# A recurrent column scan on TensorE: wrapped rows from one padded state in 32x32 tiles, and the reset product moved

## The chip, the core and the metric

The kernel is one program on one core of a Trainium2 chip. The metric is device time in microseconds: the median of three runs. TensorE is called PE, VectorE DVE, ScalarE ACT, GpSimd POOL and SyncE SP, as the profile does.

## What is computed

The input x has 16 images of 32 channels, 64 rows and 64 columns, fp32. Four residual stages follow each other; each takes the group-normalised x and adds its result to x: a 3x3 convolution, a recurrent scan over the columns, a spectral product on 16x16 modes, and a product with a full spectrum. The change touches the scan alone:

```python
def _cell(prev_col, cur_col, weight_ih, bias_ih, weight_hh, bias_hh):
    pad = jnp.pad(prev_col, ((0, 0), (1, 1), (0, 0)))
    x = jnp.concatenate([pad[:, :-2], pad[:, 1:-1], pad[:, 2:]], axis=-1)
    i_vals = jnp.einsum('bhk,ok->bho', x, weight_ih) + bias_ih
    h_vals = jnp.einsum('bhc,oc->bho', cur_col, weight_hh) + bias_hh
    r_i, z_i, n_i = jnp.split(i_vals, 3, axis=-1)
    r_h, z_h, n_h = jnp.split(h_vals, 3, axis=-1)
    r = jax.nn.sigmoid(r_i + r_h)
    z = jax.nn.sigmoid(z_i + z_h)
    n = jnp.tanh(n_i + r * n_h)
    return n * z + cur_col * (1.0 - z)
...
x = x + _L1_conv_ref(_gn(x), ...)   # 63 steps of _cell over the 64 columns
```

prev_col is the state after the column before, and each row of it is mixed with the rows above and below it.

## The kernel before

**Layout.** The 128 partitions are four quarters of 32 channels. Image row 4h+q lies in quarter q at position h, so a quarter holds 16 positions (H4) of each image. A neighbouring row is mostly in the neighbouring quarter at the same position. Only for the first and the last quarter does it wrap: row 4h-1 is in quarter 3 at position h-1, row 4h+4 in quarter 0 at position h+1.

**Two halves.** The 16 images are two halves of 8 (h = 0 and 1 in the code, HB = 128 columns each). A half step is one column for one half; there are 2 x 63 = 126, in the order (0,w), (1,w), (0,w+1). Each half has its own PSUM banks 4h to 4h+3, for r, z, the state's part of n, and the column's part of n.

**PE** (half_step, L693) runs from_column (L687) for three gates, then waits for the state, then from_state (L679) for r, n and z, each with its semaphore. Both are four matmuls of 128 rows by 32 columns a gate, one for each quarter of outputs (QUARTERS, L677), with 128 moving columns. The moving operand of quarters 1 and 2 is state; that of quarters 0 and 3 is straddled (L169): a second copy of the state with 17 places an image, whose partitions 0 to 63 are written one place off those of 64 to 127, so that one read at offset 0 or 1 holds the wrapped rows.

**The copies.** POOL writes the partitions 0 to 63 of it from mix and keep (L531), while DVE computes the same difference into state; ACT copies state's partitions 64 to 127 (L1049, state_edges) when state is there. PE's from_state waits for both (sedge_ready, lower_ready).

**DVE** (new_state, L1349) does five operations for each half step: pre1 = r gate x h part (L1352, the reset product), pre2 (L1355), keep (L1360), mix (L1363) and state = mix - keep (L1368). Its loop body has six half steps. **ACT** (scan_step, L1064) does sigmoid of r (L1054), sigmoid of z (L1058), tanh (L1062) and the copy. **POOL** also adds the state into the image (L525). **SP** brings the next column for half of the partitions (L431), once a step, when both halves have used the one before. The loop body of PE has eight half steps, that of ACT four steps.

The order on every engine is written by hand; the engines meet at semaphores only.

Of the kernel before, what the change touches and what calls it, by code (L numbers as in the profile page):

```python
# [80 lines left out]
def program(nc, x, conv_w, conv_b, scan_wi, scan_wh, scan_b, w2, w3, w9, out_b, group_d, const_d, out):  # L81
    ctx = ExitStack()
    with ctx:
        def sem(name):
            return ctx.enter_context(nc.semaphore(name))
# [61 lines left out]
        state = [scan_buf() for _ in range(2)]  # L147

# [16 lines left out]
        straddle_both = spec[:, off:off + 2 * NBR]  # L165
        straddle = [straddle_both[:, h * NBR:(h + 1) * NBR] for h in range(2)]
        off += 2 * NBR

        def straddled(h, q, first):  # L169
            return straddle[h][q].rearrange("p (b h) -> p b h", h=H4 + 1)[:, :, first:first + H4]  # L170
# [55 lines left out]
        sedge_ready = [sem(f"sedge_ready{h}") for h in range(2)]  # L226
        h_sum = [sem(f"h_sum{h}") for h in range(2)]
        lower_ready = [sem(f"lower_ready{h}") for h in range(2)]
        straddle_zeroed = sem("straddle_zeroed")
# [172 lines left out]
        def _(sp):  # L402
# [13 lines left out]
            sp.dma_start(sv[P - C:P, 0:3, 0:C], scan_wi[:, :, 2 * C:3 * C]).then_inc(scan_w_in, 16)  # L416
            sp.dma_start(sv[0:C, 0:3, P - C:P], scan_wi[:, :, 0:C]).then_inc(scan_w_in, 16)
# [67 lines left out]
        def _(pool):  # L485
# [34 lines left out]
            ROWS_01 = slice(0, P // 2)  # L520

            def add_state(h, w):
                col = image[:, h * (B // 2 * ROWS):(h + 1) * (B // 2 * ROWS)] \
                    .rearrange("p (n w) -> p n w", w=W)[:, :, ds(w, 1)]
                nc.gpsimd.tensor_tensor(col, col, state[h].unsqueeze(2), ALU.add).then_inc(added[h], 1)  # L525
# [9 lines left out]
            pool.wait_ge(straddle_zeroed, 1)  # L535
            for h in range(2):
                pool.wait_ge(state_ready[h], 1)
                nc.gpsimd.tensor_copy(straddled(h, ROWS_01, 0), state[h][ROWS_01].rearrange("p (b h) -> p b h", h=H4)
                                      ).then_inc(lower_ready[h], 1)
                add_state(h, 0)  # L540
            with pool.Fori(0, W // 2 - 1) as i:
                for k in range(2):
                    for h in range(2):
                        scan_step(h, i * 2 + (k + 1))
            for h in range(2):
                scan_step(h, W - 1)
# [58 lines left out]
        def _(pe):  # L605
# [363 lines left out]
        def _(act):  # L969
# [75 lines left out]
            ROWS_23 = slice(P // 2, P)  # L1045

            def state_edges(h, w):
                act.wait_ge(state_ready[h], w + 1)
                a(straddled(h, ROWS_23, 1), state[h][ROWS_23].rearrange("p (b h) -> p b h", h=H4),  # L1049
                  ACT.Copy).then_inc(sedge_ready[h], 1)  # L1050

# [22 lines left out]
            act.wait_ge(straddle_zeroed, 1)  # L1074
            state_edges(0, 0)
            for w in range(1, 4):
                scan_step(w)
            with act.Fori(1, W // 4) as i:
                for k in range(4):
                    scan_step(i * 4 + k)  # L1080
# [107 lines left out]
        def _(dve):  # L1188
# [131 lines left out]
            v.memset(straddle_both, 0.0).then_inc(straddle_zeroed, 1)  # L1320
# [23 lines left out]
            for h in range(2):  # L1344
                if h == 1:
                    dve.wait_ge(columns_ready, B)
                v.tensor_copy(state[h], columns[:, h * HB:h * HB + HB]).then_inc(state_ready[h], 1)

            def new_state(h, w):  # L1349
                dve.wait_ge(r_gate[h], w)  # L1350
                dve.wait_ge(h_sum[h], w)
                v.tensor_tensor(pre1[h], gr[h], psum[:, 4 * h + 3, 0:HB], ALU.mult).then_inc(reset_done[h], 1)  # L1352
                dve.wait_ge(reset_done[h], w)
# [4 lines left out]
                dve.wait_ge(lower_ready[h], w)  # L1358

# [10 lines left out]
            with dve.Fori(0, (W - 1) // 3) as i:  # L1370
                for k in range(3):
                    for h in range(2):
                        new_state(h, i * 3 + (k + 1))

# [301 lines left out]
```

## Time and profile before

| | us |
|---|---|
| median of the runs | 573.09 |
| lowest and highest | 572.53 and 574.57 |
| the profiled execution | 571.37 |
| its span, first to last instruction | 569.6 |

What lies around the span is 1.8 us. The page of the profile gives the busy time of each engine and the chain that ended last, that is, the last instruction followed back to what released it. The timeline gives single instructions; a run of equal ones is one line with its count, and its duration reaches from the first start to the last end. An fp32 matmul is two MATMUL instructions and two LDWEIGHTS (PEld). The shape behind an operation on PE (128\*32) is rows by columns of the array, the one after it the moving operand.

### The profile page before, as it was taken

What the parts mean: (1) busy time and instruction counts of PE and PEld (TensorE: products, weight loads), DVE (VectorE), ACT (ScalarE), POOL (GpSimd) and SP (SyncE); (2) the same over time, 40 slices, a digit from 0 to 9 for tenths busy, and PEclk for the clock granted to TensorE, in tenths of its full rate; (3) what the DMA queues carried; (4) which work ended last, traced back from release to release, by engine and by line L of the source; (5) the groups of instructions that cost most, each with busy time, mean ns of one, the idle gap of its engine ahead of it and who ended that gap; (6) DMA issues with size and microseconds to landing.
All of it is one profiled execution on the core that took longest, in us unless ns stands there. A gap on an engine that the chain in (4) does not pass through costs nothing.

```text
span 569.6 us, 28853 instructions
## 1 busy us (share of the span) xinstructions
PE 522.1 (92%) x11502; PEld 415.1 (73%) x11502; DVE 465.2 (82%) x1245; ACT 387.7 (68%) x814; POOL 296.0 (52%) x423
## 2 busy tenths in 40 slices
PE   2999999779999999999999999998989999999995
PEld 2333333467777777777777799997868898999995
DVE  7679885568989898989899879887877897487886
ACT  2545979867777777777777896676748998656541
POOL 7665665046666666666666520211558899522000
PEclk9999999989999999999999999999999999999999
DMA  6920000011111111111111310000308887103334
GB/s 197 412 34 0 2 2 5 1 43 40 41 42 37 46 37 42 41 38 45 37 44 39 121 41 2 1 0 2 96 25 256 264 286 251 51 1 150 148 146 151
DMA packets 26044, 45.82 MB, mean 80 GB/s; under 512 B 5632, under 2 KB 16128, under 8 KB 25104
## 3 DMA queue, kind: packets, MB, share of 16 engines
q1 hardware_dynamic: 24912, 44.98, 24.7%
q8 instruction: 32, 0.52, 0.4%
q10 hardware_dynamic: 672, 0.15, 0.1%
q0 software_dynamic: 416, 0.07, 0.1%
q14 instruction: 12, 0.10, 0.1%
HBM read 28.53 MB, written 8.39 MB: 65 GB/s over the span
## 4 chain that ended last, share of the span: by engine, by line
PE 43%; DVE 31%; issue 11%; ACT 6%; POOL 3%; DMA 3%; DVEq 2%; SPq 0%; ACTq 0%; POOLq 0%
PE psum L619 14%; PE psum L648 8%; DVE spec L1360 8%; PE psum L826 8%; DVE spec L1352 6%; DVE spec L1363 6%; PE psum L786 4%; DVE small L1245 3%; PE psum L932 3%; PE psum L747 2%; POOL work L360 2%; ACT work L302 2%; DVE spec L1355 2%; DMA image<-x_dram 1%; DVE image L1623 1%
## 5 line engine op out<-in xcount | busy, mean ns | idle before, releaser
L683 PE MATMUL psum<-spec,matrices 128*32 128x128 f32 x3024 | 109.3, 278 | 14.2 <-ACT spec L1049 7.3
L683 PEld LDWEIGHTS psum<-spec,matrices 128*32 128x32 f32 x3024 | 76.1, 110 | 46.5 <-ACT spec L1049 46.5
L690 PE MATMUL psum<-spec,matrices 128*32 128x128 f32 x3024 | 107.3, 274 | 1.3 <-DMA spec<-work 1.3
L531 POOL TENSOR_TENSOR spec<-spec 64x128 f32<-64x128 f32 x126 | 70.6, 560 | 71.9 <-DVE spec L1363 71.9
L690 PEld LDWEIGHTS psum<-spec,matrices 128*32 128x32 f32 x3024 | 85.5, 110 | 4.1 <-issue 4.0
L648 PE MATMUL psum<-spec,matrices 128*64 128x512 f32 x384 | 86.2, 606 | 1.0 <-ACT spec L983 1.0
L509 POOL TENSOR_SCALAR spec<-image,small 32x960 f32<-32x960 f32 (+1 forms) x48 | 55.6, 1159 | 34.1 <-PE psum L648 21.7
L826 PE MATMUL psum<-work 128*32 128x128 f32 x2368 | 68.9, 273 | 4.9 <-POOL work L360 2.7
L360 POOL COPY work<-work 32x768 f32<-32x768 f32 x74 | 62.2, 841 | 18.5 <-DVE work L1467 7.3
L826 PEld LDWEIGHTS psum<-work 128*32 128x32 f32 x2368 | 63.9, 110 | 9.3 <-issue 7.4
L525 POOL TENSOR_TENSOR image<-image,spec 128x128 f32 (+1 forms) x128 | 69.4, 542 | 0.0
L360 ACT ACTIVATE work<-work 32x768 f32<-32x768 f32 x74 | 62.4, 843 | 7.6 <-PE psum L826 3.1
L648 PEld LDWEIGHTS psum<-spec,matrices 128*64 128x64 f32 x384 | 27.1, 138 | 53.6 <-issue 50.5
L619 PE MATMUL psum<-kept,work 128*64 128x128 f32 x1024 | 57.0, 273 | 2.4 <-DVE work L396 1.6
L619 PEld LDWEIGHTS psum<-kept,work 128*64 128x64 f32 x1024 | 55.8, 139 | 3.1 <-ACT work L396 1.9
L1360 DVE SCALAR_TENSOR_TENSOR spec<-spec,work 128x128 f32<-128x128 f32 x126 | 54.2, 430 | 0.5 <-ACT spec L1058 0.3
L983 ACT ACTIVATE spec<-image,small 96x1024 f32<-96x1024 f32 (+1 forms) x32 | 39.5, 1234 | 18.1 <-PE psum L648 16.6
L1062 ACT ACTIVATE psum<-spec 128x128 f32<-128x128 f32 x126 | 35.5, 282 | 23.0 <-DVE spec L1355 17.3
L1355 DVE SCALAR_TENSOR_TENSOR spec<-psum,small,spec 128x128 f32<-128x128 f32 x126 | 44.2, 351 | 4.5
L1058 ACT ACTIVATE spec<-psum 128x128 f32<-128x128 f32 x126 | 35.0, 278 | 17.1 <-PE psum L683 17.0
L1054 ACT ACTIVATE spec<-psum 128x128 f32<-128x128 f32 x126 | 35.1, 279 | 15.8 <-PE psum L683 10.2
L1245 DVE BATCH_NORM_STATS2 small<-image 128x6 f32<-128x512 f32 x64 | 40.1, 682 | 5.0 <-DMA image<-x_dram 3.9
(153 smaller groups left out, 819.3 us busy)
## 6 DMA issues: line engine op xcount, KB each, us to landing
work<-w_dram SPq DMA_DIRECT2D x66, 256.0 KB, 3.3
spec<-work SPq DMA_DIRECT2D x124, 64.0 KB, 1.9
image<-x_dram SPq DMA_DIRECT2D x3, 2048.0 KB, 12.7
out_dram<-image SPq DMA_DIRECT2D x3, 2048.0 KB, 7.3
image<-x_dram SPq DMA_DIRECT2D x4, 512.0 KB, 6.0
work<-w_dram SPq DMA_DIRECT2D x1, 2048.0 KB, 8.0
out_dram<-image SPq DMA_DIRECT2D x4, 512.0 KB, 3.8
kept<-const_dram SPq DMA_DIRECT2D x1, 192.0 KB, 5.1
```

Of the source, the lines that this page charges most:

```text
L360: return copy(dst, src, *func)
L509: nc.gpsimd.tensor_scalar(to, of, sc0[j % 2][q, u:u + 1], sh0[j % 2][q, u:u + 1], ALU.mult, ALU.add).then_inc(norm_pool, 1)
L525: nc.gpsimd.tensor_tensor(col, col, state[h].unsqueeze(2), ALU.add).then_inc(added[h], 1)
L531: nc.gpsimd.tensor_tensor(straddled(h, ROWS_01, 0), *of, ALU.subtract).then_inc(lower_ready[h], 1)
L619: last = mm(out[o], stationary[:, o], moving, start=True, stop=True)
L648: last_mm = mm(psum[o, n % 4, :], cv[:, kx, o], rows_[:, 8 * half:8 * half + 8, kx:kx + W], start=kx == 0, stop=kx == 2)
L683: last = mm(psum[QUARTERS[hm], 4 * h + g, 0:HB], sv[:, g, QUARTERS[hm]], moving[hm], start=starts, stop=True)
L690: last = mm(psum[q, 4 * h + g, 0:HB], sv[:, 3 + g, q], e, start=True, stop=stops)
L826: last = mm(o, wt[t // 8][:, t % 8, r, :], pl[:, t, from_:to], start=starts and k == 0 and r == 0, stop=r == 1, skip_group_check=True)
L1245: v.bn_stats(bnv[:, at_:at_ + 6], image[:, ds(j * (GB * ROWS) + 512 * k, 512)]).then_inc(half_sem, 1)
L1355: v.scalar_tensor_tensor(out=pre2[h], in0=psum[:, 4 * h + 2, 0:HB], scalar=bias_s[:, 2:3], in1=pre1[h], op0=ALU.add, op1=ALU.add).then_inc ...
L1360: v.scalar_tensor_tensor(out=keep[h], in0=gz[h], scalar=1.0, in1=columns[:, ds(w * (2 * HB) + h * HB, HB)], op0=ALU.subtract, op1=ALU.mult ...
```

## The change

One padded state for each half replaces state and the second copy. It has 17 places an image and the places between images stay zero; each half has one place more at its front. state(h, q, group) reads it at the image's rows (group 0), one place back (-1) or one on (+1); for group +1 the view starts one place later and drops its first.

from_state then does four matmuls a gate of two shapes: two of 128x64 over all rows (the halves of the outputs, with the weights that do not wrap), and two of 32x32 for the wrapped rows, from quarter 3 to quarter 0 and from quarter 0 to quarter 3, with weights of their own in slot 7 of scan_m. All four go into the same PSUM bank. from_column does two of 128x64 a gate instead of four of 128x32.

The copies on POOL and ACT are gone, with their semaphores. DVE computes the reset product of the other half between mix and state of this half. ACT does the r and z gates of half 0 for the next step after the tanh of half 1. DVE's last three steps stand behind its loop, and so do ACT's.

```diff
-        straddle_both = spec[:, off:off + 2 * NBR]
-        straddle = [straddle_both[:, h * NBR:(h + 1) * NBR] for h in range(2)]
-        off += 2 * NBR
-
-        def straddled(h, q, first):
-            return straddle[h][q].rearrange("p (b h) -> p b h", h=H4 + 1)[:, :, first:first + H4]
+        state_both = spec[:, off:off + 2 * (NBR + 1)]
+        off += 2 * (NBR + 1)
+
+        def state(h, q=slice(0, P), group=0):
+            if group == 1:
+                at_ = h * (NBR + 1) + 1
+                return state_both[q, at_:at_ + NBR].rearrange("p (b h) -> p b h", h=H4 + 1)[:, :, 1:]
+            at_ = h * (NBR + 1)
+            return state_both[q, at_:at_ + NBR].rearrange("p (b h) -> p b h", h=H4 + 1)[:, :, 1 + group:1 + group + H4]
...
-            sp.dma_start(sv[P - C:P, 0:3, 0:C], scan_wi[:, :, 2 * C:3 * C]).then_inc(scan_w_in, 16)
-            sp.dma_start(sv[0:C, 0:3, P - C:P], scan_wi[:, :, 0:C]).then_inc(scan_w_in, 16)
+            for q, of in ((slice(P - C, P), slice(2 * C, 3 * C)), (slice(0, C), slice(0, C))):
+                sp.dma_start(sv[q, 7, 0:3 * C].rearrange("p (g c) -> p g c", c=C), scan_wi[:, :, of]).then_inc(scan_w_in, 16)
...
-            def scan_step(h, w):
-                pool.wait_ge(mix_ready[h], w)
-                pool.wait_ge(keep_ready[h], w)
-                of = [t[h][ROWS_01].rearrange("p (b h) -> p b h", h=H4) for t in (mix, keep)]
-                nc.gpsimd.tensor_tensor(straddled(h, ROWS_01, 0), *of, ALU.subtract).then_inc(lower_ready[h], 1)
-                pool.wait_ge(state_ready[h], w + 1)
-                add_state(h, w)
...
+            HALVES = (slice(0, P // 2), slice(P // 2, P))
+
             def from_state(h, g, starts=False):
 
-                moving = (straddled(h, slice(0, P), 0), state[h], state[h], straddled(h, slice(0, P), 1))
-                for hm in (1, 2, 0, 3):
-                    last = mm(psum[QUARTERS[hm], 4 * h + g, 0:HB], sv[:, g, QUARTERS[hm]], moving[hm],
-                              start=starts, stop=True)
+
+                for o in HALVES:
+                    mm(psum[o, 4 * h + g, 0:HB], sv[:, g, o], state(h), start=starts, stop=False, skip_group_check=True)
+                for to, of, group in ((0, slice(P - 32, P), -1), (3, slice(0, 32), 1)):
+                    last = mm(psum[QUARTERS[to], 4 * h + g, 0:HB], sv[of, 7, C * g:C * g + C], state(h, of, group),
+                              start=False, stop=True, skip_group_check=True)
                 return last
 
             def from_column(h, g, parity, stops=False):
-                up, lo = edges_of(h, parity)
-                for q, e in zip(QUARTERS, (up, up, lo, lo)):
-                    last = mm(psum[q, 4 * h + g, 0:HB], sv[:, 3 + g, q], e, start=True, stop=stops)
+                for o, e in zip(HALVES, edges_of(h, parity)):
+                    last = mm(psum[o, 4 * h + g, 0:HB], sv[:, 3 + g, o], e, start=True, stop=stops, skip_group_check=True)
                 return last
...
-                pe.wait_ge(sedge_ready[h], w)
-                pe.wait_ge(lower_ready[h], w)
+                pe.wait_ge(state_ready[h], w)
                 from_state(h, 0).then_inc(r_sum[h], 1)
...
-            def scan_step(w):
-                reset_gate(0, w)
-                update_gate(0, w)
-                state_edges(1, w - 1)
+            def scan_step(w, last=False):
                 candidate(0, w)
                 reset_gate(1, w)
                 update_gate(1, w)
-                state_edges(0, w)
                 candidate(1, w)
+                if not last:
+                    reset_gate(0, w + 1)
+                    update_gate(0, w + 1)
...
-            def new_state(h, w):
+            def reset(h, w):
                 dve.wait_ge(r_gate[h], w)
                 dve.wait_ge(h_sum[h], w)
                 v.tensor_tensor(pre1[h], gr[h], psum[:, 4 * h + 3, 0:HB], ALU.mult).then_inc(reset_done[h], 1)
+
+            def new_state(h, w, last=False):
+
                 dve.wait_ge(reset_done[h], w)
...
                 v.tensor_tensor(mix[h], gn[h], gz[h], ALU.mult).then_inc(mix_ready[h], 1)
+                if not last:
+                    reset(1 - h, w + h)
                 dve.wait_ge(mix_ready[h], w)
                 dve.wait_ge(keep_ready[h], w)
                 dve.wait_ge(added[h], w)
-                dve.wait_ge(sedge_ready[h], w)
-                v.tensor_tensor(state[h], mix[h], keep[h], ALU.subtract).then_inc(state_ready[h], 1)
+                v.tensor_tensor(state(h), by_image(mix[h]), by_image(keep[h]), ALU.subtract).then_inc(state_ready[h], 1)
```

## Rows read from the trace of the kernel before

**Rows 1.** Page, part 1: busy time, share of the span and instructions of each engine.
```profile
PE 522.1 (92%) x11502; PEld 415.1 (73%) x11502; DVE 465.2 (82%) x1245; ACT 387.7 (68%) x814; POOL 296.0 (52%) x423
```

**Rows 2.** Page, part 4: chain that ended last, by engine and by line.
```profile
PE 43%; DVE 31%; issue 11%; ACT 6%; POOL 3%; DMA 3%; DVEq 2%; SPq 0%; ACTq 0%; POOLq 0%
PE psum L619 14%; PE psum L648 8%; DVE spec L1360 8%; PE psum L826 8%; DVE spec L1352 6%; DVE spec L1363 6%; PE psum L786 4%; DVE small L1245 3%; PE psum L932 3%; PE psum L747 2%; POOL work L360 2%; ACT work L302 2%; DVE spec L1355 2%; DMA image<-x_dram 1%; DVE image L1623 1%
```

**Rows 3.** Views by line of L1352 and L690: duration ns minimum/median/maximum, first and last start.
```profile
L1352 DVE TENSOR_TENSOR spec<-spec,psum x126: 277/279/289, 117.1 to 320.3; 128x128 f32<-128x128 f32 x126
...
L690 PE MATMUL psum<-spec,matrices x3024: 269/273/421, 110.8 to 319.1; 128*32 128x128 f32 x189
```

**Rows 4.** Timeline of all engines, 202.4 to 206.3: start, duration, engine, line [idle before].
```profile
202.47 0.84 PE L690 MATMUL psum<-spec,matrices 128*32 128x128 f32 x24
...
202.72 0.28 DVE L1352 TENSOR_TENSOR spec<-spec,psum 128x128 f32<-128x128 f32 x1
203.02 0.31 ACT L1049 ACTIVATE spec<-spec 64x128 f32<-64x128 f32 x1
203.04 0.35 DVE L1355 SCALAR_TENSOR_TENSOR spec<-psum,small,spec 128x128 f32<-128x128 f32 x1
...
203.30 0.46 DVE L1360 SCALAR_TENSOR_TENSOR spec<-spec,work 128x128 f32<-128x128 f32 x1
...
203.38 0.86 PE L683 MATMUL psum<-spec,matrices 128*32 128x128 f32 x24
...
203.74 0.29 DVE L1363 TENSOR_TENSOR spec<-psum,spec 128x128 f32<-128x128 f32 x1
203.87 0.28 ACT L1054 ACTIVATE spec<-psum 128x128 f32<-128x128 f32 x1 [0.17 <-PE psum L683]
...
204.06 0.84 PE L690 MATMUL psum<-spec,matrices 128*32 128x128 f32 x24
204.06 0.29 DVE L1368 TENSOR_TENSOR spec<-spec 128x128 f32<-128x128 f32 x1
204.10 0.56 POOL L531 TENSOR_TENSOR spec<-spec 64x128 f32<-64x128 f32 x1 [0.49 <-DVE spec L1363]
204.27 0.28 DVE L1352 TENSOR_TENSOR spec<-spec,psum 128x128 f32<-128x128 f32 x1
...
205.61 0.29 DVE L1368 TENSOR_TENSOR spec<-spec 128x128 f32<-128x128 f32 x1
...
206.19 0.29 DVE L1352 TENSOR_TENSOR spec<-spec,psum 128x128 f32<-128x128 f32 x1 [0.30 <-issue]
```

**Rows 5.** Groups of instructions, 117 to 321: count | busy, mean ns | idle before, releasers.
```profile
L683 PEld LDWEIGHTS psum<-spec,matrices 128*32 128x32 f32 x3000 | 75.6, 110 | 42.4 <-ACT spec L1049 42.4
```

**Rows 6.** Timeline of PE, 337.9 to 346, then its first two steps alone.
```profile
338.20 7.21 PE L786 MATMUL psum<-matrices,work 128*64 128x128 f32 x128
345.34 0.46 PE L795 MATMUL psum<-matrices,work 128*32 128x32 f32 x32
...
338.20 0.44 PE L786 MATMUL psum<-matrices,work 128*64 128x128 f32 x4
```

**Rows 7.** Timeline of PE at three changes of shape: the end of the old shape.
```profile
338.00 0.27 PE L747 MATMUL psum<-kept,work 128*128 128x128 f32 x1
...
344.91 0.50 PE L786 MATMUL psum<-matrices,work 128*64 128x128 f32 x6
...
82.64 0.53 PE L667 MATMUL psum<-kept,spec 128*32 128x128 f32 x6
83.09 0.65 PE L648 MATMUL psum<-spec,matrices 128*64 128x512 f32 x2
```

**Rows 8.** Timeline of PE at the end of its loop body, 145.2 to 147.2.
```profile
145.33 0.86 PE L683 MATMUL psum<-spec,matrices 128*32 128x128 f32 x24
146.12 0.86 PE L690 MATMUL psum<-spec,matrices 128*32 128x128 f32 x24
```

**Rows 9.** Stretch 117.1 to 121.0: busy us (instructions) of each engine, granted clock, DMA.
```profile
117.10:121.00 3.90, 3.31 (x72) 3.18 (x72) 2.11 (x8) 1.46 (x6) 1.07 (x2) 0.59 0.22 53
```

More of the change, by code:

```diff
@@ L145, in scan_buf @@
             return spec[:, off - HB:off]
-        state = [scan_buf() for _ in range(2)]
         upper_e = spec[:, off:off + 4 * HB]
@@ L164, in program, with by_image @@
         NBR = B // 2 * (H4 + 1)
-        straddle_both = spec[:, off:off + 2 * NBR]
-        straddle = [straddle_both[:, h * NBR:(h + 1) * NBR] for h in range(2)]
-        off += 2 * NBR
-        def straddled(h, q, first):
-            return straddle[h][q].rearrange("p (b h) -> p b h", h=H4 + 1)[:, :, first:first + H4]
+        state_both = spec[:, off:off + 2 * (NBR + 1)]
[6 more added lines that the diff above has]
+            return state_both[q, at_:at_ + NBR].rearrange("p (b h) -> p b h", h=H4 + 1)[:, :, 1 + group:1 + group + H4]
+        def by_image(buf):
+            return buf.rearrange("p (b h) -> p b h", h=H4)
         columns = work[:, 0:B * ROWS]
@@ L225, in program @@
         state_ready = [sem(f"state_ready{h}") for h in range(2)]
-        sedge_ready = [sem(f"sedge_ready{h}") for h in range(2)]
         h_sum = [sem(f"h_sum{h}") for h in range(2)]
-        lower_ready = [sem(f"lower_ready{h}") for h in range(2)]
-        straddle_zeroed = sem("straddle_zeroed")
+        state_zeroed = sem("state_zeroed")
         r_sum, z_sum, n_sum = [[sem(f"{g}_sum{h}") for h in range(2)] for g in "rzn"]
@@ L519, in _ @@
             pool.wait_ge(norm_pool, 3 * B)
-            ROWS_01 = slice(0, P // 2)
             def add_state(h, w):
+                pool.wait_ge(state_ready[h], w + 1)
                 col = image[:, h * (B // 2 * ROWS):(h + 1) * (B // 2 * ROWS)] \
-                    .rearrange("p (n w) -> p n w", w=W)[:, :, ds(w, 1)]
-                nc.gpsimd.tensor_tensor(col, col, state[h].unsqueeze(2), ALU.add).then_inc(added[h], 1)
-            def scan_step(h, w):
-                pool.wait_ge(mix_ready[h], w)
-                pool.wait_ge(keep_ready[h], w)
-                of = [t[h][ROWS_01].rearrange("p (b h) -> p b h", h=H4) for t in (mix, keep)]
-                nc.gpsimd.tensor_tensor(straddled(h, ROWS_01, 0), *of, ALU.subtract).then_inc(lower_ready[h], 1)
-                pool.wait_ge(state_ready[h], w + 1)
-                add_state(h, w)
-            pool.wait_ge(straddle_zeroed, 1)
+                    .rearrange("p (b h w) -> p b h w", h=H4, w=W)[:, :, :, ds(w, 1)].rearrange("p b h o -> p b (h o)")
+                nc.gpsimd.tensor_tensor(col, col, state(h), ALU.add).then_inc(added[h], 1)
             for h in range(2):
-                pool.wait_ge(state_ready[h], 1)
-                nc.gpsimd.tensor_copy(straddled(h, ROWS_01, 0), state[h][ROWS_01].rearrange("p (b h) -> p b h", h=H4)
-                                      ).then_inc(lower_ready[h], 1)
                 add_state(h, 0)
@@ L543, in _ @@
                     for h in range(2):
-                        scan_step(h, i * 2 + (k + 1))
+                        add_state(h, i * 2 + (k + 1))
             for h in range(2):
-                scan_step(h, W - 1)
+                add_state(h, W - 1)
             pool.wait_ge(t_done, 8)
@@ L1042, in _ @@
                     bias=sh1[:, GB - 1:GB]).then_inc(columns_ready, 1)
[L1045 to L1050, printed above, removed]
             def reset_gate(h, w):
@@ L1070, in scan_step @@
                 update_gate(1, w)
-                state_edges(0, w)
                 candidate(1, w)
[L1074 to L1078, printed above, removed]
+                if not last:
+                    reset_gate(0, w + 1)
+                    update_gate(0, w + 1)
+            reset_gate(0, 1)
+            update_gate(0, 1)
+            with act.Fori(0, (W - 4) // 4) as i:
                 for k in range(4):
-                    scan_step(i * 4 + k)
+                    scan_step(i * 4 + (k + 1))
+            for w in range(W - 3, W):
+                scan_step(w, w == W - 1)
             act.wait_ge(added[0], W)
@@ L1319, in _ @@
             dve.wait_ge(small_in, 16 * 8)
-            v.memset(straddle_both, 0.0).then_inc(straddle_zeroed, 1)
+            v.memset(state_both, 0.0).then_inc(state_zeroed, 1)
             v.memset(bias_z, 0.0).then_inc(bias_spread, 1)
@@ L1346, in _ @@
                     dve.wait_ge(columns_ready, B)
-                v.tensor_copy(state[h], columns[:, h * HB:h * HB + HB]).then_inc(state_ready[h], 1)
-            def new_state(h, w):
+                dve.wait_ge(state_zeroed, 1)
+                v.tensor_copy(state(h), by_image(columns[:, h * HB:h * HB + HB])).then_inc(state_ready[h], 1)
+            def reset(h, w):
                 dve.wait_ge(r_gate[h], w)
@@ L1357, in new_state @@
                 dve.wait_ge(z_gate[h], w)
-                dve.wait_ge(lower_ready[h], w)
                 v.scalar_tensor_tensor(out=keep[h], in0=gz[h], scalar=1.0, in1=columns[:, ds(w * (2 * HB) + h * HB, HB)],
@@ L1366, in new_state @@
                 dve.wait_ge(added[h], w)
-                dve.wait_ge(sedge_ready[h], w)
-                v.tensor_tensor(state[h], mix[h], keep[h], ALU.subtract).then_inc(state_ready[h], 1)
-            with dve.Fori(0, (W - 1) // 3) as i:
+                v.tensor_tensor(state(h), by_image(mix[h]), by_image(keep[h]), ALU.subtract).then_inc(state_ready[h], 1)
+            reset(0, 1)
+            with dve.Fori(0, (W - 1) // 3 - 1) as i:
                 for k in range(3):
@@ L1373, in _ @@
                         new_state(h, i * 3 + (k + 1))
+            for w in range(W - 3, W):
+                for h in range(2):
+                    new_state(h, w, (h, w) == (1, W - 1))
             dve.wait_ge(added[0], W)
```

## The prediction, made before the changed kernel was run

> **What bounds the kernel now.** I start with the page. Its header counts put PE at 92% of the span, but a share is no bound [rows 1]; the chain that ended last gives PE 43% and DVE 31%, and in it four DVE lines of the scan (L1352, L1355, L1360, L1363) come to 22% [rows 2]. So some stretch is held by DVE. The first and last start of L1352 give its place: 117.1 to 320.3, 203.2 us for 126 half steps, 125 intervals of 1.626 [rows 3]. The timeline of one half step shows how it is held [rows 4]. DVE starts L1352, L1355, L1360, L1363, L1368 at 202.72, 203.04, 203.30, 203.74, 204.06 and the next L1352 at 204.27: 1.55 us with no hole. At the end of its loop body (every sixth half) the next one starts at 206.19, and 0.37 us is added: 105 x 1.55 + 20 x 1.92 = 201.2, and about 2 us more at the cold start make the 203.2. PE in the same period runs from_column in 0.91 with a wait at its end, and from_state in 0.68 (203.38 to 204.06): about 1.33 of work in 1.59. It then waits, and the wait is for ACT's copy L1049, 42 us in all over the scan [rows 5]. **The scan is bound by DVE's issue, and PE has only about 0.26 us of room per half step.** Whatever the change puts on PE beyond that is paid in full, 125 times.
>
> **What PE does per matmul.** Each fp32 matmul is two instructions: 24 for the 12 matmuls of from_state. Matmuls of all columns of the array go side by side: 24 instructions of 32 columns from 203.38 to 204.06 are six steps of four. The 128 instructions of 64 columns at L786 take 7.14 us to the start of the next shape: 64 steps of two [rows 6]. Three numbers come from there.
> - A step where the shape stays the same. The two ends of the L786 block are odd: the first step lasts 0.16 (four instructions end at 338.20 + 0.44, one takes 0.273 [rows 3 and 6], so the second pair started at 338.37), the last one 0.20. The other 62 have 7.14 - 0.36 = 6.78, so **0.109 a step**, for a whole array of 128 moving columns, whatever the cut.
> - A step at which the shape changes. In three places (128x128 to 128x64, 128x64 to 128x32, 128x32 to 128x64) the new shape starts 0.07 to 0.08 us before the last of the old one ends: 338.20 against 338.27, 345.34 against 345.41, 83.09 against 83.17 [rows 6 and 7]. Within one shape the next step starts 0.16 before that end. With 0.273 for an instruction, a change costs **0.203 for the step instead of 0.109: +0.094**.
> - The step after a change: 0.16 for 64 columns (+0.054, above). For 32 columns, from_state after a wait has 0.68 - 5 x 0.109 = 0.135 (+0.025) [rows 4].
>
> These rows agree with the Trainium skill, page TensorEngine Tiling (Array Packing), section Tiling Modes, which says that changing the tiling mode, and not just the tile, drains TensorE. That page speaks against this change.
>
> **The change on PE.** from_column becomes 2 matmuls of 128x64 a gate for 4 of 128x32: six steps as before, 0.654. from_state keeps 4 matmuls a gate, but they are no longer four column strips of one pass over the array: two of 128x64 already fill it (two steps), and the two wrapped 32x32 tiles, (rows 96-127, columns 0-31) and (rows 0-31, columns 96-127), need the same columns of the array again, with N = 128: two further steps if both run side by side. No row of before has a 32-row tile; the nearest is 32 columns, and there a step is 0.109, which I take (the moving side has the same 128 columns). So 4 steps a gate for 2: steps per half are 6 + 12 = 18, 1.962 us, for 12. Then the shape changes twice a gate, to 32x32 and back, six times a half step: 6 x 0.094 = 0.564, and behind them 3 x 0.054 + 3 x 0.025 = 0.237. **PE needs 1.962 + 0.564 + 0.237 = 2.763 us per half step.** Bounds: 1.962 if a change of shape that keeps to other rows is free, about 2.53 if only the weight load behind a change is hidden; above, 3.14 if the first and second instructions of large and small matmuls alternate (four changes a gate: 18 x 0.109 + 12 x 0.094 + 0.054), or 3.09 if the two small tiles overlap only by half (one step more a gate). Below 1.31 there is nothing; that end belongs to the rival where small tiles hide.
>
> **The change elsewhere.** All of this is beside PE, as long as PE needs over 1.6.
> - DVE: the same five operations, with the other half's reset between mix and state, so that two waits for an own result fall away. Starts that depend on the operation before are 0.32 apart (202.72 to 203.04), the independent 204.06 to 204.27 is 0.21: at best some 0.2 per half step is saved [rows 4]. It is hidden under PE's 2.76. The waits that come with it: state(h) is queued behind reset(1-h), which waits for the other half's r gate. In PE time: from_state of the other half starts at S; its r gate now has four steps (0.109 + 0.203 + 0.134, then 0.273), about 0.8 with the hop to ACT (0.49 now, 203.38 to 203.87), then sigmoid 0.28, reset, and state starts at S + 1.33 and ends at S + 1.62. PE wants that state after from_state and from_column, at S + 2.76: 1.1 us of slack, so this wait does not bind. Queued behind it are pre2, keep and mix of the other half, which wait for n_sum and z_sum of S, about then or later, anyway.
> - ACT loses L1049 (0.31 per half); its three gates need 0.84 of 2.76. POOL loses L531 (0.56) and keeps its add L525, which now reads the state with a stride of 17. Strided writes of state by DVE: even twice the 0.29 would be covered. Cover for all of it is PE; without it the DVE chain would again set the pace.
> - SP: the two corner DMAs go to slot 7, the same bytes, early. The column DMAs wait for both h_sum and have 5.5 us per step where now 3.2 do.
> - The first memset is 2 columns longer: nothing. The first half step loses an ACT copy and a POOL copy, under 1 us, inside the cold start.
>
> **The sum.** First to last L1352 after: 125 x 2.763 = 345.4. PE's loop edge, now half hidden: from_state takes 0.79 for 0.68 there (145.33 to 146.12) [rows 8], taken as 0.13 x 15 = 2.0. The clock is at its lower level (1.2 of 2.4 GHz) for part of the first 3.9 us, mean 0.59 [rows 9]; work bound by PE loses 3.9 x 0.41 = 1.6 there. Together 349.0, for 203.2 now: +145.8. At the end of the scan z's last step starts 1.85 after the last from_state (0.649 + 0.703 + 0.163 + 0.203 + 0.134) and ends at 2.13, and with sigmoid, tanh, mix and state (0.28, 0.28, 0.32, 0.29 and the hops) that is 3.4 us instead of 2.5 (203.38 to 205.90): +0.9. **+146.7 us.** The profiled execution has 571.37, which gives 718.1; the median of the runs is 573.09, 1.7 above it, and that gives **719.8**.
>
> **Rivals.**
> 1. *Changing shape is free here* (the 32x32 tiles are seen as parts of the same cut). 1.962 per half: 245.3 + 2.0 + 1.6 - 203.2 + 0.5 = +46, **619**. Against it: every change of shape in the rows pays, 64 to 32 columns among them. Part of it free (the load behind it hidden) is 2.53, about 690, within my main case; an effect of one direction only would give about 660.
> 2. *Large and small alternate instruction by instruction, or the small ones do not pair*: 3.09 to 3.14, 125 x 0.33 to 0.38 more than the forecast, **760 to 767**. The rows show that equal neighbours run in steps of four or two with their first instructions together, so some interleaving exists; whether it reaches across shapes they can't show.
> 3. *Small tiles hide beside the large ones* and PE needs 12 steps, 1.31. Then the loop state, PE, r gate, reset of the other half, state decides: 0.29 + 0.05 + 0.49 + 0.28 + 0.03 + 0.21 = 1.35 for 1.55 now, 125 x 0.2 = 25 less, **548, faster**. It decides from the point at which PE's work per half is below 1.55, that is less than 0.24 us for all six small tiles and changes. For it speaks only that four strips of 32 columns share one step; against it, that the two large tiles cover all rows and columns. The Trainium skill, page TensorE: Matmul & The Clock Gate, Part 3, has 32x32 tiles at different positions overlap with a few ns between their starts; by that rule, if it held beside larger tiles, this rival would be the outcome. No row here has 32-row tiles.
> 4. That the change does not do what it says (the reset not between, the copies still there) is not open: the diff moves the instructions themselves.
>
> **How the numbers follow.** Forecast (690 to 730) 0.60; rival 2 0.14; between rival 1 and the forecast 0.08; rival 1 0.12; rival 3 0.06. The range 640 to 772 holds the forecast, rival 2 and the in-between, 0.82, and leaves out rivals 1 and 3. Faster by over 0.5% (about what a measurement of this kernel can tell from no change) is rival 3: 0.06; within 0.5%: 0.01; slower: 0.93.
>
> **What would show it.** In the profile after: PE without waits for ACT or DVE in the scan, L1352's starts 2.76 apart, from_state 128x64 and 32x32 groups in turn with 0.20 between the last of one and the first of the other, 0.109 within; sigmoid of r about 0.8 after from_state starts; DVE idle about half of the time, waiting for PE. If steps of the small tiles were shorter than 0.109, or overlapped with large ones, I am too high; if the granted clock falls in the scan, too low.

## The result, and the profile after

| | before | changed |
|---|---|---|
| median of the runs, us | 573.25 | 751.63 |
| lowest and highest, us | 572.53 and 574.57 | 737.66 and 767.88 |
| profiled execution, us (span) | 571.37 (569.6) | 737.66 (735.9) |
| its granted clock over the span | 0.995 | 0.963 |

The ratio is 1.295, with a 95% interval of 1.282 to 1.309: slower by 29.5%, where +25.6% was forecast. The ratios here and in the table of experiments compare only the runs that lie near the fastest of their kernel (here 737.66 and 748.49); the two medians as they stand give 1.311, that is +31.1%. The four runs of the changed kernel lie 30 us apart, and they do so in the order of PE's mean granted clock (0.963, 0.947, 0.935, 0.918 for 737.66, 748.49, 754.78, 767.88). The profile below is the fastest of them. The median before, 573.25, is of four runs; 573.09 is that of three of them.

The page of the changed kernel first: busy time, PE's clock in 40 slices, the chain by engine and by line. They answer to [rows 1] and [rows 2].

```profile
PE 701.9 (95%) x9990; PEld 478.3 (65%) x9990; DVE 447.0 (61%) x1245; ACT 336.4 (46%) x687; POOL 230.7 (31%) x295
...
PEclk9999996559999999999999999999999999999999
...
PE 82%; DVE 7%; ACT 5%; issue 2%; POOL 2%; DMA 1%; DVEq 0%; SPq 0%; POOLq 0%; ACTq 0%
PE psum L678 18%; PE psum L676 17%; PE psum L684 15%; PE psum L610 11%; PE psum L639 6%; PE psum L819 5%; PE psum L779 3%; DVE small L1230 3%; PE psum L925 2%; PE psum L740 2%; ACT work L305 2%; ACT work L363 2%; POOL work L363 1%; PE psum L605 1%; DVE image L1615 1%
```

The three matmul lines of the scan, L678 (32x32), L676 (128x64 from the state) and L684 (from_column), now hold half of the span, where the scan's DVE lines held 22%. DVE went from 31% of the chain to 7%. And PEclk shows 6, 5, 5 from 110 to 166 us of the span, where the scan starts; before, it was:

```profile
PEclk9999999989999999999999999999999999999999
```

These are two separate effects: what a half step costs, and the clock at the start of the scan.

**The half step.** The timeline of PE over one half step (start, duration, engine, line, shape, count):

```profile
250.03 0.39 PE L684 MATMUL psum<-spec,matrices 128*64 128x128 f32 x4
250.25 0.39 PE L676 MATMUL psum<-spec,matrices 128*64 128x128 f32 x4
250.56 0.41 PE L678 MATMUL psum<-spec,matrices 32*32 32x128 f32 x4
250.90 0.44 PE L676 MATMUL psum<-spec,matrices 128*64 128x128 f32 x4
251.27 0.41 PE L678 MATMUL psum<-spec,matrices 32*32 32x128 f32 x4
251.61 0.44 PE L676 MATMUL psum<-spec,matrices 128*64 128x128 f32 x4
251.98 0.41 PE L678 MATMUL psum<-spec,matrices 32*32 32x128 f32 x4
252.32 0.88 PE L684 MATMUL psum<-spec,matrices 128*64 128x128 f32 x12
253.03 0.28 PE L676 MATMUL psum<-spec,matrices 128*64 128x128 f32 x2
```

from_state starts at 250.25 and the next one at 253.03: 2.78 us, with no wait for DVE or ACT. The gates stand 0.65, 0.71 and 0.71 apart, and from_column takes 0.71; the prediction's steps give 0.649, 0.703, 0.703 and 0.708. The instruction counts show how two matmuls of a shape share their steps: the small pair is 4 instructions in 0.41, that is two steps, 0.13 between their starts and 0.28 for the last to end. The changes of shape are the gaps from the start of a group's second step to the start of the next group: the second step of the group at 250.25 starts at 250.36 (0.28 before its end at 250.64), the small group at 250.56, so 0.20 here.

On the other engines, in the same stretch (the idle time before an operation and what ended it, in brackets):

```profile
250.08 0.29 DVE L1347 SCALAR_TENSOR_TENSOR spec<-spec,work 128x128 f32<-128x128 f32 x1 [0.69 <-ACT spec L1044]
250.29 0.29 DVE L1350 TENSOR_TENSOR spec<-psum,spec 128x128 f32<-128x128 f32 x1
...
251.02 0.28 ACT L1040 ACTIVATE spec<-psum 128x128 f32<-128x128 f32 x1 [0.77 <-PE psum L678]
...
251.33 0.29 DVE L1338 TENSOR_TENSOR spec<-spec,psum 128x128 f32<-128x128 f32 x1 [0.75 <-ACT spec L1040]
251.54 0.29 DVE L1356 TENSOR_TENSOR spec<-spec 128x128 f32<-128x128 f32 x1
```

The r gate's sigmoid starts 0.77 after from_state (251.02 for 250.25; 0.8 was worked out). The other half's reset product (L1338) comes between mix (L1350) and state (L1356) as the diff says, and waits there 0.75 us. State ends at 251.83, 1.58 us after that from_state started, and PE asks for it 2.78 after: the wait that came with the new order binds nothing. Where before DVE had no hole in a half step [rows 4], it now stands idle for half of it.

**The clock.** Two waits of PE at the start of the scan, three stretches of it (length, busy us and instructions of PE, PEld, DVE, ACT, POOL, then the granted clock, DMA share and GB/s), and the reset product's first and last start, to be set against [rows 3] and [rows 9]:

```profile
113.84 0.44 PE L676 MATMUL psum<-spec,matrices 128*64 128x128 f32 x4 [1.67 <-DVE spec L1333]
...
118.15 1.55 PE L684 MATMUL psum<-spec,matrices 128*64 128x128 f32 x12 [0.94 <-DMA spec<-work]
...
114.00:118.00 4.00, 3.21 (x24) 1.15 (x22) 0.95 (x4) 3.51 (x6) 1.03 (x2) 0.53 0.07 16
118.00:160.00 42.00, 41.85 (x312) 23.82 (x312) 11.28 (x43) 6.43 (x26) 4.37 (x8) 0.50 0.07 17
168.00:484.00 316.00, 316.00 (x4102) 189.66 (x4100) 151.09 (x570) 84.00 (x341) 62.12 (x114) 1.00 0.10 23
...
L1338 DVE TENSOR_TENSOR spec<-spec,psum x126: 286/289/290, 117.2 to 484.6; 128x128 f32<-128x128 f32 x126
```

A half step has 36 matmul instructions. From 118 to 160 there are 312, that is 8.7 half steps of 4.85 us, at the lower level of 1.2 GHz; from 168 on one takes 2.77 at 2.4 GHz. In the kernel before, the clock was low in the scan only within the first 3.9 us [rows 9]. From the first to the last L1338 it is 367.3 us; 125 x 2.777 are 347.1, and the low stretch is the other 20. In the trace it lasts 51 us, from 114.2 to 165.4.

### The profile page after: what moved, and what is told of

Same layout as the page of the kernel before. It is cut to its first block, busy times and chain, and to the rows that moved or that the text cites. A ratio compares the mean times of both kernels' runs of the same rounds, so it can differ in the third digit from the quotient of the medians.

```text
span 735.9 us, 25048 instructions
## 1 busy us (share of the span) xinstructions
PE 701.9 (95%) x9990; PEld 478.3 (65%) x9990; DVE 447.0 (61%) x1245; ACT 336.4 (46%) x687; POOL 230.7 (31%) x295
## 4 chain that ended last, share of the span: by engine, by line
PE 82%; DVE 7%; ACT 5%; issue 2%; POOL 2%; DMA 1%; DVEq 0%; SPq 0%; POOLq 0%; ACTq 0%
PE psum L678 18%; PE psum L676 17%; PE psum L684 15%; PE psum L610 11%; PE psum L639 6%; PE psum L819 5%; PE psum L779 3%; DVE small L1230 3%; PE psum L925 2%; PE psum L740 2%; ACT work L305 2%; ACT work L363 2%; POOL work L363 1%; PE psum L605 1%; DVE image L1615 1%
## 5 line engine op out<-in xcount | busy, mean ns | idle before, releaser
L676 PE MATMUL psum<-spec,matrices 128*64 128x128 f32 x1512 | 167.7, 302 | 1.7 <-DVE spec L1333 1.7
L678 PE MATMUL psum<-spec,matrices 32*32 32x128 f32 x1512 | 161.5, 291 | 0.0
L676 PEld LDWEIGHTS psum<-spec,matrices 128*64 128x64 f32 x1512 | 85.7, 142 | 56.1 <-issue 54.2
L684 PE MATMUL psum<-spec,matrices 128*64 128x128 f32 x1512 | 117.1, 293 | 0.9 <-DMA spec<-work 0.9
L684 PEld LDWEIGHTS psum<-spec,matrices 128*64 128x64 f32 x1512 | 85.1, 143 | 27.8 <-issue 27.7
L1338 DVE TENSOR_TENSOR spec<-spec,psum 128x128 f32<-128x128 f32 x126 | 36.3, 288 | 108.6 <-ACT spec L1040 108.6
L678 PEld LDWEIGHTS psum<-spec,matrices 32*32 32x32 f32 x1512 | 54.0, 105 | 69.7 <-issue 69.7
L1347 DVE SCALAR_TENSOR_TENSOR spec<-spec,work 128x128 f32<-128x128 f32 x126 | 36.8, 292 | 85.9 <-ACT spec L1044 85.9
L639 PEld LDWEIGHTS psum<-spec,matrices 128*64 128x64 f32 x384 | 27.2, 139 | 53.8 <-issue 50.5
```

The lines of the kernel that those rows point to most:

```text
L639: last_mm = mm(psum[o, n % 4, :], cv[:, kx, o], rows_[:, 8 * half:8 * half + 8, kx:kx + W], start=kx == 0, stop=kx == 2)
L676: mm(psum[o, 4 * h + g, 0:HB], sv[:, g, o], state(h), start=starts, stop=False, skip_group_check=True)
L678: last = mm(psum[QUARTERS[to], 4 * h + g, 0:HB], sv[of, 7, C * g:C * g + C], state(h, of, group), start=False, stop=True, skip_group_check ...
L684: last = mm(psum[o, 4 * h + g, 0:HB], sv[:, 3 + g, o], e, start=True, stop=stops, skip_group_check=True)
L1347: v.scalar_tensor_tensor(out=keep[h], in0=gz[h], scalar=1.0, in1=columns[:, ds(w * (2 * HB) + h * HB, HB)], op0=ALU.subtract, op1=ALU.mult ...
```

## Experiments

Every kernel was timed in turns with the kernel before on the same chip (573.9 to 574.6 us there). Half steps are the mean distance of the reset product's starts in the second half of the scan.

| run | median us | ratio (95%) | half step | clock |
|---|---|---|---|---|
| e1_grouped | 652.40 | 1.140 (1.134 to 1.146) | 2.237 | 0.995 |
| e2_no_small | 546.72 | 0.953 (0.949 to 0.957) | 1.398 | 0.993 |
| e3_no_small_old_order | 574.86 | 1.003 (1.001 to 1.005) | 1.618 | 0.993 |
| e4_one_cut | 617.68 | 1.076 (1.073 to 1.079) | 1.969 | 0.995 |
| e5_old_order | 732.92 | 1.273 (1.266 to 1.280) | 2.777 | 0.901 |
| e6_warm | 718.62 | 1.252 (1.247 to 1.258) | 2.777 | 0.996 |
| e7_small_pair | 598.78 | 1.043 (1.039 to 1.047) | 1.795 | 0.990 |
| e8_same_pair | 574.93 | 1.001 (0.998 to 1.004) | 1.612 | 0.991 |
| e9_body_7 | 572.93 | 0.997 (0.9945 to 0.9997) | 1.60 | 0.991 |

The clock is that of the profiled execution; for e5_old_order that was the slowest of its five runs, 781.5 us.

### Steps or changes of shape: e1_grouped and e4_one_cut

The changed kernel with the small matmuls of all three gates behind the large ones (from_state keeps the large ones alone):

```diff
+            def wrapped(h, g):
                 for to, of, group in ((0, slice(P - 32, P), -1), (3, slice(0, 32), 1)):
...
-                from_state(h, 0).then_inc(r_sum[h], 1)
-                from_state(h, 2, True).then_inc(n_sum[h], 1)
-                from_state(h, 1).then_inc(z_sum[h], 1)
+                from_state(h, 0)
+                from_state(h, 2, True)
+                from_state(h, 1)
+                wrapped(h, 0).then_inc(r_sum[h], 1)
+                wrapped(h, 2).then_inc(n_sum[h], 1)
+                wrapped(h, 1).then_inc(z_sum[h], 1)
```

> The changed kernel with its matmuls in another order: in each half step the large (128x64) matmuls of all three gates first, then the small (32x32) ones of all three. As many steps of PE as before, but the shape changes twice a half step and not six times. Theory (PE's steps and its changes of shape are the time): 18 x 0.109 + 2 x 0.094 + 0.054 + 0.025 = 2.23 us a half step instead of 2.78; 571.4 - 203.2 + 125 x 2.23 + 1.6 + 1 = about 649 us, more if PE's clock is low for longer than 3.9 us. Rival (the small matmuls are themselves slow, the change of shape is not): 2.78 again, 718 or more. Second rival (the later r gate now decides: state 0.29, hop 0.05, r group 1.2, sigmoid 0.31, reset to state 0.21): 2.1, below PE's 2.23, so not seen.

The timeline of PE in e1_grouped:

```profile
249.86 0.83 PE L676 MATMUL psum<-spec,matrices 128*64 128x128 f32 x12
250.62 0.85 PE L680 MATMUL psum<-spec,matrices 32*32 32x128 f32 x12
251.40 0.88 PE L686 MATMUL psum<-spec,matrices 128*64 128x128 f32 x12
252.10 0.82 PE L676 MATMUL psum<-spec,matrices 128*64 128x128 f32 x12
```

2.24 us a half step (249.86 to 252.10), 2.237 on average: the same instructions as in the changed kernel, in another order, and 0.54 less. Four changes of shape fewer, so 0.135 for each, of which the prediction had 0.094 in the step and 0.054 or 0.025 in the one behind it. That the small matmuls are slow in themselves is out: e1_grouped has as many of them. The kernel takes 652.4 us for 649.

And with one shape everywhere; the weights of the wrapped rows are padded with zeros over all 128 rows, and from_column has its four matmuls of 128x32 a gate as before. In from_state:

```diff
...
+                for q in QUARTERS:
+                    mm(psum[q, 4 * h + g, 0:HB], sv[:, g, q], state(h), start=starts, stop=False, skip_group_check=True)
+                for i, (to, group) in enumerate(((0, -1), (3, 1))):
+                    at_ = 7 * P + 3 * C * i + C * g
+                    last = mm(psum[QUARTERS[to], 4 * h + g, 0:HB], scan_m[:, at_:at_ + C], state(h, slice(0, P), group),
+                              start=False, stop=True, skip_group_check=True)
```

> The changed kernel with every matmul of the scan in one shape, 128x32: four for the rows that don't wrap, two for the wrapped ones (weights padded with zeros over 128 rows, read from the same padded state one place back or on). As many steps of PE as the changed kernel, no change of shape. Theory: 18 x 0.109 = 1.962 us a half step: 571.4 - 203.2 + 245.3 + 1.6 + 0.5 = 616 us. Rival (a small matmul hides part of a step that a full one does not): the half step is above 1.962 by that part, up to 2.78 if the steps themselves were the whole cost.

1.969 us a half step for 1.962, and 617.7 us for 616. It computes the same as the changed kernel, with no change of shape, and is 0.81 us a half step shorter: 2.777 - 1.969 = 0.808, over six changes 0.135 each, the same price as from e1_grouped. What is left above the kernel before, 1.969 for 1.61, is six more steps over the array (0.65 us) less PE's room (0.26): 0.39 by these numbers, 0.36 measured. The three half steps, 1.969, 2.237 and 2.777 with none, two and six changes, lie on one line; so a 32x32 tile costs the array as much time as a 128x32 one full of zeros.

### What the rest of the change is worth: e2 and e3

e2_no_small drops the loop over the small matmuls in from_state, so it leaves the wrapped rows out of the computation. e3_no_small_old_order does that and puts the reset product back:

```diff
             def new_state(h, w, last=False):
 
+                reset(h, w)
                 dve.wait_ge(reset_done[h], w)
...
-                if not last:
-                    reset(1 - h, w + h)
...
-            reset(0, 1)
```

> The changed kernel without its small matmuls: the wrapped rows are left out of the computation. PE has 12 steps a half step, 1.31 us. Theory: the rest of the change is a gain that PE hides; the loop state, PE, r gate, reset of the other half gives 1.35 us a half step and 20 loop edges of DVE at about 0.37: 571.4 - 25 = about 546 to 550 us. Rival (the new order of DVE or the strided state costs something of its own): 571 us or more.

> The changed kernel without its small matmuls (wrapped rows left out of the computation) and with DVE's old order: the reset product of a half first in its own half step. Theory: DVE's issue sets the pace again as in the kernel before, 1.55 us a half step and the loop edges: 569 to 572 us. The difference to the run without small matmuls in the new order is what the moved reset product is worth: about 22 to 25 us. Rival (the missing copies alone are worth the gain): both runs equal, near 548.

546.7 and 574.9 us. With PE at 12 steps the new order makes the kernel 4.7% faster than the one before; with the old order everything else in the change together (no copies, the padded state, 128x64 tiles) brings nothing, if anything a loss of 0.3%. So the moved reset product is worth 28 us, (1.618 - 1.398) x 125 = 27.5, and only where PE lets it. Whether it would be worth that with the copies still there was not tried. DVE in e2_no_small and, below, in e3_no_small_old_order:

```profile
200.87 0.29 DVE L1334 TENSOR_TENSOR spec<-spec,psum 128x128 f32<-128x128 f32 x1
201.08 0.29 DVE L1352 TENSOR_TENSOR spec<-spec 128x128 f32<-128x128 f32 x1
201.29 0.34 DVE L1340 SCALAR_TENSOR_TENSOR spec<-psum,small,spec 128x128 f32<-128x128 f32 x1
201.55 0.28 DVE L1343 SCALAR_TENSOR_TENSOR spec<-spec,work 128x128 f32<-128x128 f32 x1
201.98 0.29 DVE L1346 TENSOR_TENSOR spec<-psum,spec 128x128 f32<-128x128 f32 x1 [0.15 <-ACT psum L1044]
202.22 0.29 DVE L1334 TENSOR_TENSOR spec<-spec,psum 128x128 f32<-128x128 f32 x1
```

```profile
201.07 0.29 DVE L1347 TENSOR_TENSOR spec<-psum,spec 128x128 f32<-128x128 f32 x1
201.40 0.29 DVE L1351 TENSOR_TENSOR spec<-spec 128x128 f32<-128x128 f32 x1
201.60 0.28 DVE L1334 TENSOR_TENSOR spec<-spec,psum 128x128 f32<-128x128 f32 x1
201.92 0.35 DVE L1341 SCALAR_TENSOR_TENSOR spec<-psum,small,spec 128x128 f32<-128x128 f32 x1
202.19 0.37 DVE L1344 SCALAR_TENSOR_TENSOR spec<-spec,work 128x128 f32<-128x128 f32 x1
202.62 0.29 DVE L1347 TENSOR_TENSOR spec<-psum,spec 128x128 f32<-128x128 f32 x1
```

In the new order reset, state and pre2 start 0.21 apart; in the old one mix to state and reset to pre2 are 0.33 and 0.32 apart. 1.35 us for 1.55 in these rows.

The same question on the changed kernel itself, PE holding:

> The changed kernel with DVE's old order (each half's reset product in its own half step), everything else as changed. Theory: PE holds 2.78 us a half step and hides DVE's order: the same half step at full clock within 0.01 us, so the same time as the changed kernel but for the clock (715 at a clock as in the kernel before, up to 768 as its runs were). Rival (the wait of state for the other half's reset binds): shorter by up to 0.2 us a half step, 25 us.

Its half step is 2.777 us, to the nanosecond that of the changed kernel: neither the gain nor the new wait of the reordering is to be seen. The median (732.9, runs from 723 to 782, the slowest above the 768 that were expected at most) is the clock's, below.

### The clock: e6_warm

```diff
+                if nth is None and h == 0:
+                    for _ in range(20):
+                        mm(psum[:, 4, 0:P], group_m, group_m, start=True, stop=True)
                 pe.wait_ge(state_ready[h], w)
                 from_state(h, 0).then_inc(r_sum[h], 1)
```

> The changed kernel with 20 further matmuls (128x128, result unused) where PE waits for the first state before the first from_state. Theory (PE's idle time there lets its clock fall to the lower level, and the pattern of short gaps after it keeps it low for 50 us and more): the clock stays at its upper level, 1.0 in all stretches of the scan, 2.78 us for every half step and about 713 to 717 us, with runs closer together. Rival (the pattern of the scan itself, with a drained array six times a half step, lets the clock fall): the clock falls all the same, 735 to 768.

718.6 us for 713 to 717, the four runs within 3.6 us. The 20 matmuls take 4.7 us, longer than the wait that they fill, so PE no longer waits for the first state. The same stretches in e6_warm:

```profile
114.00:118.00 4.00, 4.00 (x43) 2.77 (x44) 0.87 (x3) 2.24 (x4) 0.55 (x1) 1.00 0.19 47
118.00:160.00 42.00, 42.00 (x550) 25.33 (x550) 19.91 (x75) 11.36 (x47) 8.21 (x15) 1.00 0.11 27
...
L1341 DVE TENSOR_TENSOR spec<-spec,psum x126: 286/288/289, 116.8 to 463.9; 128x128 f32<-128x128 f32 x126
```

The clock does not fall, and the scan takes 347.1 us from its first to its last reset product. So it is PE's idle time at the start of the scan that brings it down, and not the pattern of the scan. In the changed kernel the clock falls at 114.2, right behind the wait of 1.67 us before the first from_state; in the profiled execution of e5_old_order it falls at 117.1, inside the wait for the column's DMA, 2.1 us there and 0.94 in the changed kernel. In e6_warm PE waits at neither place, so which of the two waits would be enough alone is not shown. But once the clock was low, it stayed low for long in this pattern: 51 us in the changed kernel, 150 us in the profiled execution of e5_old_order, with PE busy in the records but for the DMA wait. Of e5_old_order, then of e1_grouped:

```profile
118.00:260.00 142.00, 142.00 (x1056) 79.81 (x1058) 41.79 (x147) 21.38 (x87) 15.76 (x29) 0.50 0.06 15
272.00:528.00 256.00, 256.00 (x3322) 153.46 (x3318) 131.35 (x461) 68.20 (x277) 50.57 (x93) 1.00 0.10 23
...
118.00:160.00 42.00, 42.00 (x654) 35.00 (x656) 22.18 (x88) 14.73 (x54) 11.51 (x17) 0.97 0.13 32
```

In their profiled executions e1_grouped (two changes a half step) and e4_one_cut (none) fall at the start of the scan as well, at 117.4 and 118.7, and are back after 3.4 us; e7_small_pair (two) and e8_same_pair (none) are back after 6.8.

The four runs of the changed kernel bear out what the low clock costs: since the rows show two levels alone, (1 - mean clock) x 2 x span is the time at the lower one over the whole execution, 54 us in the fastest run and 126 us in the slowest, and a microsecond at that level loses 1 - 2.777 / 4.86 = 0.43: 31 us between the two, where 30.2 were measured.

That the changes of shape are what delays the return fits these rows, but is not shown. By the same formula the nine runs of the changed kernel and e5_old_order have 20 to 154 us at the lower level, and all other runs of the experiments, the kernel before among them, 3 to 24, but for one: a run of e9_body_7, whose scan has one shape, took 613.0 us at a mean clock of 0.850, that is 183 us. So a long low stretch came without changes of shape too, if rarely; where in that run it lay is not on record. Why the scan's pattern is enough to hold the upper level and mostly not to regain it soon was not settled.

### PE's room in the kernel before: e7 and e8

```diff
                 from_column(h, 0, parity)
+                for q in (slice(0, 32), slice(P - 32, P)):
+                    mm(psum[q, 4 * h + 3, 256:256 + HB], sv[q, 7, 0:C], bias_z[q], start=True, stop=True)
                 from_column(h, 1, parity)
```

e8_same_pair has sv[:, 7, 0:C] and bias_z there, all 128 rows, the shape of its neighbours.

> The kernel before with one pair of 32x32 matmuls added to each half step, between the first and the second gate of from_column; their result goes to unused PSUM. They add two steps and two changes of shape to PE: 2 x 0.109 + 2 x 0.094 + 0.05 = 0.456 us, where PE has 0.26 us of room. Theory: PE becomes the bound at 1.335 + 0.456 = 1.79 us a half step for 1.626 with loop edges: +20 us, 592. Rival (small tiles hide beside others, or a change of shape is free): at most 0.22 of added work, inside the room, 573.

> The kernel before with one pair of 128x32 matmuls (the shape of all others in the scan) added to each half step at the same place, result unused. Two steps, 0.218 us, no change of shape; PE has 0.26 us of room. Theory: hidden, 573 to 575 us. Rival (PE's room is smaller than the timeline shows, since the wait of from_state for the copy is what ends it): up to +0.22 us a half step, 600.

One pair of small tiles costs 24.5 us, one pair of full ones 0.6, which is nothing (interval 0.998 to 1.004). PE in e7_small_pair:

```profile
250.73 0.43 PE L690 MATMUL psum<-spec,matrices 128*32 128x128 f32 x8
251.09 0.41 PE L703 MATMUL psum<-spec,matrices 32*32 32x128 f32 x4
251.43 0.64 PE L690 MATMUL psum<-spec,matrices 128*32 128x128 f32 x16
251.89 0.84 PE L683 MATMUL psum<-spec,matrices 128*32 128x128 f32 x24
252.54 0.40 PE L690 MATMUL psum<-spec,matrices 128*32 128x128 f32 x8
```

1.79 us a half step was worked out, 1.795 is measured. Of the 4.5 us above the expected 20, 2 to 3 come from the subtraction: 1.626 for the kernel before holds the slow start of the scan, and 1.79 does not; over the second half of the scan the kernel before takes 1.610, and 125 x (1.795 - 1.610) is 23. The rest was not traced.

### A version that might beat both: e9_body_7

```diff
-            with dve.Fori(0, (W - 1) // 3) as i:
-                for k in range(3):
+            with dve.Fori(0, (W - 1) // 7) as i:
+                for k in range(7):
                     for h in range(2):
-                        new_state(h, i * 3 + (k + 1))
+                        new_state(h, i * 7 + (k + 1))
```

> The kernel before with DVE's scan loop in 9 turns of 14 half steps instead of 21 turns of 6. At each loop edge DVE loses 0.37 us in the trace of the kernel before. Theory (the edge is a fixed price): 12 edges fewer, -4.4 us, 569 us where the kernel before has 573.5. Rival (the edge is dearer for a longer body, or PE and ACT then fill what DVE leaves): 573.

572.9 us for 574.6: 0.3% faster, and the interval (0.9945 to 0.9997) only just leaves out 1. Eleven of the twelve runs lie between 569.6 and 575.2; the twelfth is the one of 613.0 above. Twelve edges are gone, but in the profiled execution the eight that are left cost about 0.42 instead of 0.37, and nearly half of the other half steps take 1.59 instead of 1.55, so more than half of the 4.4 us comes back; what holds them was not taken apart. It is the only one that computes everything and is at all faster than the kernel before, so no version that clearly beats it was found. A from_state in 64x32 tiles, rows 0 to 63 and 64 to 127 apart, was not tried.

## Why the prediction was right

The mechanism was right, and so was the half step (2.763 us for 2.777 measured); the time is right with some luck. The median of 751.6 lies above 690 to 730, the band of the forecast with its chance of 0.60. It lies within 640 to 772 only because that range left room for rival 2, and rival 2 did not happen: what filled the room is the clock, which the prediction names in its last sentence as a sign of being too low and gives, beyond the first 3.9 us, neither a price nor a chance.

- **What bound the kernel** (DVE's issue, 1.55 us, and PE with 0.26 us of room): right. e8_same_pair puts 0.22 us of steps into that room for nothing, e7_small_pair 0.456 and pays the excess, 1.795 for 1.79.
- **18 steps of 0.109** (1.962): e4_one_cut measures 1.969. The step taken over from 128x32 for a tile of 32 rows, the one term without a row of before, held (by the line through e4_one_cut, e1_grouped and the changed kernel).
- **Six changes of shape** (0.564 and 0.237 behind them, 0.80): 0.808 from e4_one_cut, 0.54 for four of them from e1_grouped (0.53 by the same numbers). The rows behind this were changes of column width; it holds for a change of rows too. The Trainium skill (TensorEngine Tiling (Array Packing), section Tiling Modes) says that a change of tiling mode drains the array; all of these agree, and 0.135 us is its price here.
- **2.763 a half step**: 2.777.
- **The cover** (the reordering hidden, the wait of state not binding): e5_old_order, no difference; the moved reset product is worth 28 us without the cover (e2 against e3), where 25 were worked out. With it rival 3 is priced: 548 given, 546.7 measured, had the small tiles been free.
- **Rival 1** (619) is what e4_one_cut has, 617.7: steps without changes. **Rival 2** did not come: the small pair shares its two steps, and large and small do not alternate instruction by instruction.
- **The term that was mis-sized is the clock at the start.** I had 3.9 us at a mean of 0.59 as in the kernel before, 1.6 us of loss; the profiled execution had 51 us at the lower level, about 21 of loss, and other runs up to 126 us over the whole execution. That is nearly all of the 19.6 us between 718.1 and the profiled 737.66, and more in the median. I had seen the fall in [rows 9] and asked only what the same 3.9 us would cost a PE that is bound, not whether the new pattern would end it as soon. With the clock held up (e6_warm) the kernel takes 718.6 for a forecast of 719.8. How long the low stretch lasts, and so where between 737.7 and 767.9 a run ends, stays open.
- Two small terms were off, one each way: the 2.0 us for PE's loop edges did not show (half steps of 2.77 to 2.78 at the upper level all along; the durations read for it, 0.79 and 0.68, would give 0.11 an edge and 1.7 us), and the end of the scan cost about 2 us and not 0.9 (251.3 us from the last reset product to the end of the span, for 249.3).

## What to carry to other kernels

Before matmuls are cut into smaller tiles, count PE's passes over the array and the changes of tile shape in the order of issue: a small tile takes the array's time of a large one with as many moving columns, and each change costs a little more than a further step (0.135 us for 0.109 here). If shapes must mix, group them, or pad the small weights with zeros to the shape of the neighbours. A gain on one engine is worth what the next engine's room allows, here 0.26 us a half step, and that room can be measured beforehand by adding a matmul whose result nobody reads. And where PE's clock falls in a wait, do not count on the return that it had under other work: filling the wait took away the risk here (718.6 us for 751.6).

## What the runs showed of the hardware that was not expected

- A PE that is busy in nearly every record can stay at the lower clock for 51 us (the changed kernel) or 150 us (e5_old_order), with six changes of shape in 18 steps, while the same work at the upper level stays there for over 300 us (e6_warm). In profiled executions with two changes or none it was back after 3.4 to 6.8 us; one run of e9_body_7, without any, had 183 us at the lower clock.
- At the lower clock this pattern takes 4.86 us a half step, 1.75 times and not twice the 2.777.
- A pair of 32x32 tiles in opposite corners of the array share their steps: their first instructions start together, and their second ones together 0.13 us later, as those of two 128x64 tiles do after 0.11 (0.16 behind a change).
